# Score stacks with heads' rows interleaved by four, and the third key stack copied over its whole width

## The chip, the cores and the metric

The kernel runs on one core of a Trainium2 chip. A core has TensorE (PE, matmuls), VectorE (DVE), ScalarE (ACT), GpSimd (POOL) and SyncE (SP, which here only issues DMAs), each with its own instruction stream; they meet at semaphores. On-chip data lies in SBUF, in 128 partitions (rows); PE writes its results to PSUM, eight banks of 128 rows by 512 floats. The metric is the device time of one execution in microseconds, lower being better.

## The reference

Four graph layers follow each other over x of shape (8, 1024, 256) with a dense 1024 by 1024 adjacency per batch element; each is x = x + layer(relu(layernorm(x)), adj). The change touches only the second, eight-head attention with a head width of 32, whose scores are multiplied by twice the adjacency ahead of the softmax:

```
q, k, v = (proj(Wq, bq), proj(Wk, bk), proj(Wv, bv))      # (b, 8 heads, 1024, 32)
scores = jnp.einsum('bhqd,bhkd->bhqk', q, k) * SCALE       # SCALE = 32 ** -0.5
mask = (adj_matrix + bond_matrix)[:, None, :, :]           # both are adj
scores = scores * mask
attn = jax.nn.softmax(scores, axis=-1)
ctx = jnp.einsum('bhqk,bhkd->bhqd', attn, v)
```

All of it is float32.

## The kernel before

The program loops over the eight batch elements (batches 0 to 7); each runs the four layers in turn, with all weights and the batch's x in SBUF. Every engine has its instructions written out in order by hand; nothing is planned at run time. What follows is layer two.

**Projections.** Queries and keys are computed transposed: 128 rows of a "group" (four heads of 32 rows) by 512 columns (one half of the 1024 nodes). There are two groups and two halves, so eight projections (`project_kq`, in the order of `KQ`). ACT rounds each to the short float format that PE multiplies fast (`khi`, `qhi`), and DVE writes what is missing, again in that format (`klo`, `qlo`, `lower_kq`, L725). Semaphore `lo_s` counts the latter.

**Stacks.** A head's 32 rows don't fill PE's 128. The kernel puts four blocks of 32 rows above each other: `kS` holds khi, khi, klo, klo, and `qS` holds qhi, qlo, qhi, qlo, so that one matmul over 128 rows sums all four products of high and low parts. A head's place j in its group is head mod 4 (`HPG` is 4). For places 0, 1 and 2 the stacks are filled by DMA, from SBUF to SBUF, all issued by SP in `stack` (L446): four copies per stack (one per block), each for both groups (heads j and 4 + j) and one half of the nodes, 32 rows by 2 by 512 floats, 128 KB. For place 3 (heads 3 and 7) PE does it instead: the matrices `pick` (built once by DVE, L603) select and repeat rows in matmuls, and ACT copies the result (`LASTS`, L979).

**Order on SP, per batch:** wait for `lo_s` 2; keys (half 0) of places 0 and 1; wait for 5; keys (half 1) of place 0; wait for 6; queries (half 0) of place 0; keys (half 1) of place 1; queries (half 0) of place 1; keys of place 2, half 0, then half 1; queries (half 0) of place 2; wait for 8; queries (half 1) of places 0 to 3. That is 52 copies. Each stack has a semaphore that reaches 64 when its four copies have landed.

**Units.** A unit u is one tile of 128 queries and one head: 64 units, in the order of heads 3, 7, 0, 4, 1, 5, 2, 6 within each tile. `scores(u)` (L1202) is two matmuls of 128 by 512. In the first tile it waits for its stacks; heads 3 and 7 need no DMA, heads 0, 1 and 2 (units 2, 4, 6) wait for theirs, and heads 4, 5, 6 come with them. It also waits until DVE has read the scores of unit u - 2, which stood in the same two banks. DVE multiplies the scores by the adjacency and takes the maximum (`Z`, L787), POOL negates it (L545), ACT takes the exponential (L1002), PE transposes (L1224), ACT and DVE copy that out of PSUM (L992, L742), and PE weighs the values four heads at a time (L1252). Beside the first units PE also does two late query projections and the value projections (`BESIDE`), which ACT copies (L983). The last query projection stands behind unit 4's scores, and DVE's `lower_kq` of it ahead of DVE's `Z` of unit 4; a value projection stands behind unit 6's scores.

Of the kernel before, what the change touches and what calls it, by code (L numbers as in the profile page):

```python
# [5 lines left out]
F32 = mybir.dt.float32  # L6
# [5 lines left out]
P = 128  # L12
# [19 lines left out]
def build_program(nc, x_in, adj_in, adjT_in, mask_in, wqkT0, wv0, w1attn, bq1, bk1, bv1, bo1,  # L32
                  w1T, b1, gamma, beta, w2T, b2, w3attn, bq3, bk3, bv3, out):
    B, N, D = x_in.shape
    NT = N // P
    DT = D // P
    NH = N // HALF
# [4 lines left out]
    HD = D // HEADS  # L42
    HPG = P // HD
# [18 lines left out]
    with ctx:  # L62
# [3 lines left out]
        def signal(name, per):  # L66
            return Signal(ctx.enter_context(nc.semaphore(name)), per)
# [3 lines left out]
        ident = sb("ident", [P, P])  # L71
# [11 lines left out]
        pick = sb("pick", [P, 4, P], F32R)  # L83
# [61 lines left out]
        qS, kS = a1  # L145
# [18 lines left out]
        khi, klo, qhi, qlo, hT1, W1 = p1a  # L164
# [35 lines left out]
        x_in_s = signal("x_in_s", 32)  # L200
        out_s = signal("out_s", 16)
        x_free = signal("x_free", 1)
        kS_in = [[signal(f"kS_in{s}{j}", 64) for j in range(HPG - 1)] for s in range(NH)]
        qS_in = [[signal(f"qS_in{s}{j}", 64) for j in range(HPG - 1 + s)] for s in range(NH)]
        last_ps = signal("last_ps", len(LASTS))
        lasts = signal("lasts", len(LASTS))
# [192 lines left out]
        @block.sync  # L399
        def _(sp):  # L400
            def load(dst, src):
                sp.dma_start(dst, src).then_inc(weights_in.sem, 16)

            def load_x(b):
                sp.dma_start(xn[:], x_in[bass.ds(b, 1)].rearrange("o (t p) d -> p (o t) d", p=P)).then_inc(x_in_s.sem, 16)
                sp.dma_start(mask[:], mask_in[bass.ds(b, 1)].rearrange("o p t -> p (o t)")).then_inc(x_in_s.sem, 16)

            def load_adj(b):
                sp.dma_start(adjN[:], adj_in[bass.ds(b, 1)].rearrange("o (t p) n -> p (o t) n", p=P)).then_inc(adj_in_s.sem, 16)

            def load_w1():
                for i in range(3):
                    sp.dma_start(W1[:, i], w1attn[i].rearrange("(t p) d -> p t d", p=P)).then_inc(w1_in.sem, 16)

            def load_adjT(b):
                sp.dma_start(adjT[:], adjT_in[bass.ds(b, 1)].rearrange("o (t p) n -> p (o t) n", p=P)).then_inc(adjT_in_s.sem, 16)


            sp.sem_inc(x_free.sem, 1)
            load_x(0)  # L420
            sp.dma_start(wqk0s[:], wqkT0.rearrange("(t p) d -> p t d", p=P)).then_inc(weights0_in.sem, 16)
            sp.dma_start(W0[:, :, D:2 * D], wv0.rearrange("(t p) d -> p t d", p=P)).then_inc(weights0_in.sem, 16)
            for dst, src in ((gammac, gamma), (betac, beta), (bv1c, bv1), (bq3c, bq3), (bk3c, bk3), (bq1c, bq1),
                             (bk1c, bk1)):
                load(dst[:], src)
            load(w2s[:], w2T.rearrange("(t p) d -> p t d", p=P))
            load(Wo1[:], w1attn[3].rearrange("(t p) d -> p t d", p=P))
            for i in range(2):
                load(w3s[:, i], w3attn[i].rearrange("(t p) d -> p t d", p=P))
            for dst, src in ((bo1B, bo1), (b2B, b2), (bv3B, bv3)):  # L430
                load(dst[:], src.partition_broadcast(P))
            load_adjT(0)
            load_w1()
            load_adj(0)
            sp.wait_ge(m3_made.sem, 1)
            sp.dma_start(M3_kept, M3s[:]).then_inc(m3_kept.sem, 16)
            sp.wait_ge(m3_kept.sem, 16)

            def batch(b, last):


                def stack(dst, parts, j, cols, done):

                    for r, src in enumerate(parts):
                        to = dst[HD * r:HD * r + HD].rearrange("p (g j) n -> p g j n", j=HPG)[:, :, j, cols]
                        sp.dma_start(to.bitcast(F32), src[HD * j:HD * j + HD, :, cols].bitcast(F32)).then_inc(done.sem, 16)  # L446

                def stack_k(s, j):
                    stack(kS, (khi, khi, klo, klo), j, half(s), kS_in[s][j])

                def stack_q(s, j):
                    stack(qS, (qhi, qlo, qhi, qlo), j, half(s), qS_in[s][j])


                sp.wait_ge(*lo_s(b, 2))
                stand(sp, waited_sp)
                stack_k(0, 0)
                stack_k(0, 1)
                sp.wait_ge(*lo_s(b, 5))
                stand(sp, waited_sp)  # L460
                stack_k(1, 0)
                sp.wait_ge(*lo_s(b, 6))
                stand(sp, waited_sp)
                stack_q(0, 0)
                stack_k(1, 1)
                stack_q(0, 1)
                stack_k(0, 2)
                stack_k(1, 2)
                stack_q(0, 2)
                sp.wait_ge(*lo_s(b, 8))  # L470
                stand(sp, waited_sp)
                for j in range(HPG):
                    stack_q(1, j)

                def reload_adjT(part):
                    tiles = slice(BACK[part].start, BACK[part].stop)
                    sp.dma_start(adjT[:, tiles], adjT_in[bass.ds(b, 1)].rearrange("o (t p) n -> p (o t) n", p=P)[:, tiles]).then_inc(adjT_back[part].sem, 16)

                sp.wait_ge(*pv_ps(b, NT * GROUPS - 1))
                stand(sp, waited_sp)  # L480
                reload_adjT(0)
                sp.wait_ge(*T_ps(b, 2 * UNITS))
                stand(sp, waited_sp)
                reload_adjT(1)
                sp.wait_ge(*ctxs(b, NT))
                stand(sp, waited_sp)
                reload_adjT(2)
                sp.wait_ge(*adjT_back[2](b, 16))
                stand(sp, waited_sp)
                sp.dma_start(wB[:], adj_in[bass.ds(b, 1)][0, 0].partition_broadcast(P)).then_inc(wB_in.sem, 16)  # L490
                sp.dma_start(W1h[:], w1T.rearrange("(t p) d -> p t d", p=P)).then_inc(w2_in.sem, 16)
                sp.dma_start(W2g[:], w2T.rearrange("(t p) d -> p t d", p=P)).then_inc(w2_in.sem, 16)
                sp.dma_start(b1B[:], b1.partition_broadcast(P)).then_inc(w2_in.sem, 16)
                if not last:
                    load_w1()
                sp.wait_ge(*a3_ps(b, NT))
                stand(sp, waited_sp)
                sp.dma_start(M3[:], M3_kept).then_inc(w3_in.sem, 16)
                sp.dma_start(W3v[:, :, 0:D], w3attn[2].rearrange("(t p) d -> p t d", p=P)).then_inc(w3_in.sem, 16)
                if not last:  # L500
                    load_x(b + 1)
                    load_adj(b + 1)

                    sp.wait_ge(*p3s(b, NH * NT))
                    stand(sp, waited_sp)
                    load_adjT(b + 1)
                sp.wait_ge(*x3s(b, NT))
                stand(sp, waited_sp)
                sp.dma_start(out[bass.ds(b, 1)].rearrange("o (t p) d -> p (o t) d", p=P), x[:]).then_inc(out_s.sem, 16)
                sp.wait_ge(*out_s(b, 16))  # L510
                sp.sem_inc(x_free.sem, 1)

            with sp.Fori(0, B - 1) as b:
                batch(b, False)
            batch(B - 1, True)


# [81 lines left out]
        def _(dve):  # L599
            dve.wait_ge(consts_ready.sem, 5)  # L600
            for i, blocks in enumerate(((0, 1), (2, 3), (0, 2), (1, 3))):
                for r in range(P // HD):
                    dve.tensor_scalar(pick[:, i, HD * r:HD * (r + 1)], ident[:, P - HD:P], float(r in blocks), None,  # L603
                                      ALU.mult).then_inc(picks.sem, 1)

            def statistics(b, l, t, src):
# [466 lines left out]
        def _(pe):  # L1073
# [43 lines left out]
            def batch(b):  # L1117
# [73 lines left out]
                def scores(u):  # L1191
                    t, hd = u // HEADS, ORDER[u % HEADS]
                    if u >= 2:
                        pe.wait_ge(*zs(b, u - 1))
                    j = hd % HPG
                    if hd < HPG - 1 and t == 0:
                        for s in range(NH):
                            pe.wait_ge(*kS_in[s][j](b, 64))
                    if hd < len(qS_in[t // TPH]) and t % TPH == 0:
                        pe.wait_ge(*qS_in[t // TPH][j](b, 64))  # L1200
                    for s in range(NH):
                        mm = pe.matmul(ps[:, 2 * (u % 2) + s], qS[:, hd, rows(t)], kS[:, hd, half(s)], start=True, stop=True)  # L1202
                    mm.then_inc(S_ps.sem, 1)
# [67 lines left out]
                for u in range(STEPS):  # L1271
# [9 lines left out]
                    if u in BESIDE:  # L1281
                        what, n = BESIDE[u]
# [133 lines left out]
                for n in range(NH * NT):  # L1416
                    s, kt = n // NT, n % NT
# [4 lines left out]
                for t in range(NT):  # L1422
                    s, a = t // TPH, t % TPH
# [45 lines left out]
```

## Time and profile before

| | us |
|---|---|
| median of 3 runs | 3081.29 (3079.47 to 3081.74) |
| profiled execution, its own time | 3079.83 |
| its span, first to last instruction | 3078.0 |
| PE busy | 2976.1 (97%) |
| PE weight loads busy | 2353.4 (76%) |
| DVE busy | 1893.0 (61%) |
| ACT busy | 1473.6 (48%) |
| POOL busy | 692.9 (23%) |

Busy time is the sum of the times of an engine's instructions; PE's matmuls overlap, and their ends are modelled. Of the chain of waits that ended last, 68% of the span is PE's and 5% SP's. The hardware queue of DMAs moved 199.96 MB; 416 of its transfers are stack copies of 128 KB, 52 in each batch.

### The profile page before, as it was taken

What the parts mean: (1) busy time and instruction counts of PE and PEld (TensorE: products, weight loads), DVE (VectorE), ACT (ScalarE), POOL (GpSimd) and SP (SyncE); (2) the same over time, 40 slices, a digit from 0 to 9 for tenths busy, and PEclk for the clock granted to TensorE, in tenths of its full rate; (3) what the DMA queues carried; (4) which work ended last, traced back from release to release, by engine and by line L of the source; (5) the groups of instructions that cost most, each with busy time, mean ns of one, the idle gap of its engine ahead of it and who ended that gap; (6) DMA issues with size and microseconds to landing.
All of it is one profiled execution on the core that took longest, in us unless ns stands there. A gap on an engine that the chain in (4) does not pass through costs nothing.

```text
span 3078.0 us, 63372 instructions
## 1 busy us (share of the span) xinstructions
PE 2976.1 (97%) x22896; PEld 2353.4 (76%) x22896; DVE 1893.0 (61%) x4170; ACT 1473.6 (48%) x2729; POOL 692.9 (23%) x1241
## 2 busy tenths in 40 slices
PE   7999999999999999999999999999999999999999
PEld 6687786877878777788777887778867788677886
DVE  2698426984269742787437874378643786438863
ACT  1684217833178331783327833277322773238722
POOL 0243002430024300242002420034200342013410
PEclk9999999999999999999999999999999999999999
DMA  4302213022130231302313013121132212221200
GB/s 169 90 2 90 76 70 90 2 90 86 59 90 2 90 108 44 84 3 89 131 30 75 19 73 131 39 66 45 58 119 53 52 59 66 97 67 38 80 8 14
DMA packets 98905, 204.35 MB, mean 66 GB/s; under 512 B 11024, under 2 KB 42128, under 8 KB 98576
## 3 DMA queue, kind: packets, MB, share of 16 engines
q1 hardware_dynamic: 98576, 199.96, 20.9%
q8 instruction: 206, 3.38, 0.4%
q14 instruction: 123, 1.01, 0.1%
HBM read 136.75 MB, written 8.65 MB: 47 GB/s over the span
## 4 chain that ended last, share of the span: by engine, by line
PE 68%; issue 11%; DVE 8%; SPq 5%; POOL 4%; ACT 3%; DMA 1%; DVEq 0%; POOLq 0%; ACTq 0%
PE ps L1077 37%; PE ps L1300 11%; PE ps L1224 7%; SPq L446 4%; PE ps L1372 4%; PE ps L1252 4%; PE ps L1202 3%; POOL H L557 3%; DVE Z L787 2%; DVE stats L608 1%; DVE h L845 1%; PE ps L1114 1%; POOL nm L545 1%; ACT Z L1002 1%; DMA qS<-qlo 1%
## 5 line engine op out<-in xcount | busy, mean ns | idle before, releaser
L787 DVE CUSTOM_DVE_ANT_0 Z<-ps,adjN 128x1024 f32<-128x1024 f32 x512 | 623.8, 1218 | 69.9 <-PE ps L1202 69.9
L1002 ACT ACTIVATE Z<-Z,nm 128x1024 f32<-128x1024 f32 x512 | 587.1, 1147 | 66.7 <-POOL nm L545 66.7
L1224 PE MATMUL ps<-ident,Z 128*128 128x128 f32 x4096 | 547.8, 277 | 26.5 <-ACT Z L1002 17.6
L1224 PEld LDWEIGHTS ps<-ident,Z 128*128 128x128 f32 x4096 | 459.7, 141 | 139.3 <-issue 64.1
L1202 PE MATMUL ps<-kS,qS 128*128 128x512 f32 x1024 | 372.1, 446 | 28.4 <-DMA qS<-qlo 28.4
L534 POOL TENSOR_SCALAR ve<-mv 128x4 f32<-128x4 f32 x80 | 15.7, 196 | 1340.1 <-DVE mv L613 1339.4
L557 POOL TENSOR_SCALAR H<-adjN 128x128 fp32r<-128x128 f32 (+1 forms) x456 | 316.8, 695 | 0.0
L545 POOL TENSOR_TENSOR nm<-nm,minus 128x1 f32<-128x1 f32 x512 | 97.1, 190 | 767.4 <-DVE nm L787 762.8
L1077 PE MATMUL ps<-mh,adjT 128*128 128x256 f32 x1024 | 223.6, 379 | 0.0
L1077 PE MATMUL ps<-v,P 128*128 128x257 f32 x1024 | 223.6, 379 | 0.0
L1077 PE MATMUL ps<-hT,t3T 128*128 128x512 f32 x512 | 221.0, 592 | 0.0
L1077 PEld LDWEIGHTS ps<-v,P 128*128 128x128 f32 x1024 | 193.8, 189 | 31.9 <-issue 3.8
L1077 PEld LDWEIGHTS ps<-mh,adjT 128*128 128x128 f32 x1024 | 193.9, 190 | 26.0
L742 DVE COPY PTa<-ps 128x512 f32<-128x512 f32 x256 | 175.8, 687 | 31.9 <-PE ps L1224 31.9
L1202 PEld LDWEIGHTS ps<-kS,qS 128*128 128x128 f32 x1024 | 161.1, 192 | 39.7 <-DVE nm L787 20.4
L1077 PEld LDWEIGHTS ps<-hT,t3T 128*128 128x128 f32 x512 | 97.3, 190 | 119.1 <-issue 118.6
L1077 PE MATMUL ps<-W,hT 128*128 128x256 f32 x768 | 186.4, 395 | 0.0
L682 DVE CUSTOM_DVE_ANT_0 E<-ps,G 128x256 f32<-128x256 f32 x64 | 27.2, 424 | 245.1 <-PE ps L1077 211.0
L992 ACT ACTIVATE PTb<-ps 128x512 f32<-128x512 f32 x256 | 144.2, 588 | 59.4 <-PE ps L1224 59.4
L1077 PEld LDWEIGHTS ps<-W,hT 128*128 128x128 f32 x768 | 149.7, 200 | 25.8
L992 ACT ACTIVATE PTa<-ps 128x512 f32<-128x512 f32 x256 | 150.4, 588 | 39.1 <-PE ps L1224 39.1
L1061 ACT ACTIVATE E<-ps,cj 128x512 f32<-128x512 f32 x128 | 87.9, 687 | 159.6 <-PE ps L1077 159.6
(170 smaller groups left out, 5673.5 us busy)
## 6 DMA issues: line engine op xcount, KB each, us to landing
adjT<-adjT_in SPq DMA_DIRECT2D x8, 4096.0 KB, 13.1
adjN<-adj_in SPq DMA_DIRECT2D x8, 4096.0 KB, 17.3
adjT<-adjT_in SPq DMA_DIRECT2D x8, 2048.0 KB, 9.1
qS<-qhi SPq DMA_DIRECT2D x112, 128.0 KB, 2.5
qS<-qlo SPq DMA_DIRECT2D x112, 128.0 KB, 2.5
kS<-khi SPq DMA_DIRECT2D x96, 128.0 KB, 2.4
kS<-klo SPq DMA_DIRECT2D x96, 128.0 KB, 2.5
adjT<-adjT_in SPq DMA_DIRECT2D x8, 1536.0 KB, 12.0
```

Of the source, the lines that this page charges most:

```text
L446: sp.dma_start(to.bitcast(F32), src[HD * j:HD * j + HD, :, cols].bitcast(F32)).then_inc(done.sem, 16)
L545: pool.tensor_tensor(nm[:, u:u + 1], nm[:, u:u + 1], minus[:], ALU.mult).then_inc(nms.sem, 1)
L557: done = pool.tensor_scalar(H[:, t, of], adjN[:, t, of], 0.0, 0.0, ALU.is_equal, ALU.is_equal)
L742: dve.tensor_copy(PT(u)[:, NT // 2:NT], heads_of(ps[:, bank])).then_inc(PT_dve.sem, 1)
L787: dve.tensor_tensor_reduce(Z[:, u % ZS], ps[:, 2 * (u % 2):2 * (u % 2) + 2].rearrange("p a n -> p (a n)"), adjN[:, u // HEADS], SCORE_SCAL ...
L992: act.activation(PT(u)[:, first:first + NT // 2], heads_of(ps[:, bank]), ACT.Copy).then_inc(PT_act.sem, 1)
L1002: act.activation(Z[:, u % ZS], Z[:, u % ZS], ACT.Exp, bias=nm[:, u:u + 1], accum_out=sm[:, u:u + 1]).then_inc(exps.sem, 1)
L1077: mm = pe.matmul(dst, lhsT, rhs, start=(i == 0), stop=(i == len(pairs) - 1))
L1202: mm = pe.matmul(ps[:, 2 * (u % 2) + s], qS[:, hd, rows(t)], kS[:, hd, half(s)], start=True, stop=True)
L1224: mm = pe.transpose(ps[:, turn_bank((u, s)), rows(a)], Z[:, u % ZS, rows(NT // 2 * s + a)], ident[:])
L1252: mm = pe.matmul(ps[HD * j:HD * j + HD, 7, P * (g % GROUPS):P * (g % GROUPS + 1)], v[:, kt, HD * hd:HD * hd + HD], PT(HPG * g + j)[:, kt], ...
L1300: mm = pe.matmul(dst(n, i), lhs(n, j, i), rhs(n, j, i), start=(j == 0 and i == 0), stop=(j == NT - 1 and i == 0))
```

## The change

The rows of `wq1`, `wk1` and their biases' outputs are permuted within each group of 128: output row 4 d + j now holds dimension d of the head at place j, where row 32 j + d held it. A head's rows are thus j, j + 4, j + 8 and so on. In the stacks, block r takes the rows r, r + 4, ... in the same way. The copies step over rows by four at both ends, `pick` is written with the same step, and every stack has each head's dimensions in the same order of rows for keys and queries. The two halves of place 2's keys become one set of four copies of 32 rows by 2 by 1024 floats, 256 KB each, with one semaphore; a batch then issues 48 copies.

```
-        kS_in = [[signal(f"kS_in{s}{j}", 64) for j in range(HPG - 1)] for s in range(NH)]
+        kS_in = [[signal(f"kS_in{s}{j}", 64) for j in range(HPG - 1 - s)] for s in range(NH)]
@@ stack, on SP
                     for r, src in enumerate(parts):
-                        to = dst[HD * r:HD * r + HD].rearrange("p (g j) n -> p g j n", j=HPG)[:, :, j, cols]
-                        sp.dma_start(to.bitcast(F32), src[HD * j:HD * j + HD, :, cols].bitcast(F32)).then_inc(done.sem, 16)
+                        to = dst[r:P:HPG].rearrange("p (g j) n -> p g j n", j=HPG)[:, :, j, cols]
+                        sp.dma_start(to.bitcast(F32), src[j:P:HPG, :, cols].bitcast(F32)).then_inc(done.sem, 16)
@@ batch, on SP
                 stack_q(0, 0)
                 stack_k(1, 1)
                 stack_q(0, 1)
-                stack_k(0, 2)
-                stack_k(1, 2)
+                stack(kS, (khi, khi, klo, klo), HPG - 2, slice(0, N), kS_in[0][HPG - 2])
                 stack_q(0, 2)
@@ pick, on DVE
-                    dve.tensor_scalar(pick[:, i, HD * r:HD * (r + 1)], ident[:, P - HD:P], float(r in blocks), None,
+                    dve.tensor_scalar(pick[:, i, r:P:HPG], ident[:, HPG - 1:P:HPG], float(r in blocks), None,
                                       ALU.mult).then_inc(picks.sem, 1)
@@ scores, on PE
                         for s in range(NH):
-                            pe.wait_ge(*kS_in[s][j](b, 64))
+                            if j < len(kS_in[s]):
+                                pe.wait_ge(*kS_in[s][j](b, 64))
@@ kernel
+    def interleaved(a):
+
+        a = np.asarray(a)
+        return np.swapaxes(a.reshape(-1, P // 32, 32), -1, -2).reshape(a.shape)
+
-        "wq1": T(L1_gnn_Wq), "wk1": T(L1_gnn_Wk), "wv1": T(L1_gnn_Wv),
+        "wq1": interleaved(T(L1_gnn_Wq)), "wk1": interleaved(T(L1_gnn_Wk)), "wv1": T(L1_gnn_Wv),
-        "bq1": columns(L1_gnn_bq), "bk1": columns(L1_gnn_bk),
+        "bq1": columns(interleaved(L1_gnn_bq)), "bk1": columns(interleaved(L1_gnn_bk)),
```

## Rows read from the trace of the kernel before

**Rows 1.** The page, part 1: busy time, share and instructions of each engine
```profile
PE 2976.1 (97%) x22896; PEld 2353.4 (76%) x22896; DVE 1893.0 (61%) x4170; ACT 1473.6 (48%) x2729; POOL 692.9 (23%) x1241
```

**Rows 2.** Waits of PE over the span: total us, times, longest us
```profile
PE ps L1202 <- DMA qS<-qlo: 28.4, 16, 2.3
```

**Rows 3.** Chain of waits, 482 to 500 us: start us, us, what
```profile
491.81 2.65 DMA qS<-qlo
```

**Rows 4.** Timeline of SP, batch 1: start us, us, issue
```profile
473.60 1.25 SPq L446 DMA_DIRECT2D kS<-khi  x2
...
484.08 0.64 SPq L446 DMA_DIRECT2D qS<-qlo  x1
484.76 1.24 SPq L446 DMA_DIRECT2D kS<-khi  x2
...
491.81 0.60 SPq L446 DMA_DIRECT2D qS<-qlo  x1
```

**Rows 5.** Issues of qS, M3, adjN: duration ns min/median/max; and landings of qS
```profile
L446 SPq DMA_DIRECT2D qS<-qhi x112: 585/598/1553, 97.7 to 2781.4; - x112
DMA to landing us min/median/max: 2.3/2.5/4.0
L498 SPq DMA_DIRECT2D M<-M_kept x8: 338/339/339, 326.1 to 2986.2; - x8
L409 SPq DMA_DIRECT2D adjN<-adj_in x8: 372/838/2775, 20.6 to 2608.8; - x8
```

**Rows 6.** Timeline of PE, batch 1: start us, us, what, idle before
```profile
486.68 0.70 PE L1202 MATMUL ps<-kS,qS 128*128 128x512 f32 x2 [1.43 <-DMA qS<-qlo]
...
491.26 1.09 PE L1224 MATMUL ps<-ident,Z 128*128 128x128 f32 x8 [0.81 <-DVE PTa L742]
494.60 1.19 PE L1202 MATMUL ps<-kS,qS 128*128 128x512 f32 x2 [2.24 <-DMA qS<-qlo]
...
499.03 0.71 PE L1202 MATMUL ps<-kS,qS 128*128 128x512 f32 x2
```

**Rows 7.** Windows: us; busy PE, PEld, DVE, ACT, POOL; clock; DMA share; GB/s
```profile
110.00:120.00 10.00, 7.08 (x41) 5.46 (x40) 6.33 (x11) 5.16 (x9) 0.57 (x3) 1.00 0.84 193
490.00:500.00 10.00, 6.94 (x32) 5.46 (x32) 6.61 (x12) 4.72 (x9) 0.57 (x3) 0.83 0.87 201
870.00:880.00 10.00, 7.21 (x27) 5.99 (x28) 5.32 (x10) 4.03 (x8) 0.57 (x3) 0.66 0.87 201
```

**Rows 8.** Timeline of PE, batch 0 and then batch 2
```profile
116.40 0.70 PE L1202 MATMUL ps<-kS,qS 128*128 128x512 f32 x2 [2.10 <-DMA qS<-qlo]
...
119.45 0.72 PE L1202 MATMUL ps<-kS,qS 128*128 128x512 f32 x2
873.88 1.19 PE L1202 MATMUL ps<-kS,qS 128*128 128x512 f32 x2 [2.13 <-DMA qS<-qlo]
...
879.80 0.48 PE L1202 MATMUL ps<-kS,qS 128*128 128x512 f32 x1
```

**Rows 9.** Timeline of SP: first stack copies of batches 1 and 2
```profile
467.13 1.31 SPq L446 DMA_DIRECT2D kS<-khi  x2
846.78 1.29 SPq L446 DMA_DIRECT2D kS<-khi  x2
```

**Rows 10.** Timeline of ACT and of DVE behind unit 4's scores, batch 1
```profile
489.14 0.69 ACT L973 ACTIVATE qhi<-ps,bq1c 128x512 fp32r<-128x512 f32 x1 [2.51 <-PE ps L1077]
491.12 1.21 DVE L787 CUSTOM_DVE_ANT_0 Z<-ps,adjN 128x1024 f32<-128x1024 f32 x1
```

**Rows 11.** Windows, batch 1: stack copies, then the adjacency load
```profile
476.00:493.00 17.00, 14.11 (x71) 10.23 (x69) 9.30 (x16) 10.25 (x19) 0.95 (x5) 1.00 0.84 194
767.00:777.00 10.00, 10.00 (x47) 8.70 (x46) 2.74 (x9) 1.79 (x4) 0.00 (x0) 1.00 0.98 386
```

**Rows 12.** Groups by line: the instructions that write pick
```profile
L603 DVE TENSOR_SCALAR pick<-ident 128x32 fp32r<-128x32 f32 x16 | 1.5, 174 | 1.7 <-POOL minus L526 1.7
```

## The prediction

> **What bounds the kernel now.** I read the busy times first. PE is busy 2976.1 us of 3078.0 [rows 1], so only what PE waits for, or a lower clock, can give much back. The list of PE's waits is headed by one: the scores' matmuls wait for the copy that fills the query stack, 28.4 us in 16 waits, two in each of the eight batches [rows 2]. The chain of waits around the second of them (batch 1; batches count from 0) runs through SP's issues one after another, then 2.65 us of a DMA, then PE [rows 3]. SP's own timeline shows why: from 473.60 to 491.81 us it issues copies with 0.04 us between them, each taking about 0.60 us, so one every 0.643 us [rows 4, 5]. PE at that place has two waits [rows 6]: unit 4's scores (head 1, start 486.68, after 1.43 us idle) for the copies of `stack_q(0, 1)`, and unit 6's scores (head 2, start 494.60, after 2.24 us idle) for `stack_q(0, 2)`. I call them S4 and S6, and S7 the next unit's.
>
> Two things follow S6. First the clock: in ten microseconds around S6 the granted clock is 1.00 in batch 0, 0.83 in batches 1, 3, 5, 6 and 7, and 0.66 in batches 2 and 4 [rows 7]; that is 3.4 or 6.8 us at the lower level (1.2 instead of 2.4 GHz), which begins after PE has idled 0.81 us and then 2.24 us within a few microseconds. From S6 to S7 batch 0 takes 119.45 - 116.40 = 3.05 us, batch 1 499.03 - 494.60 = 4.43 us, batch 2 879.80 - 873.88 = 5.92 us [rows 6, 8]. So a short low stretch costs 1.38 us and a long one 2.87 us. Second, nothing behind S7 absorbs a delay: from S7 to the next batch's first stack copy it is 467.13 - 119.45 = 347.68 us in batch 0 and 846.78 - 499.03 = 347.75 us in batch 1 [rows 6, 8, 9]. Whatever S7 gains, the batch gains, one for one.
>
> **The third key stack over its whole width.** Eight issues of 128 KB (heads of place 2, two halves of four) become four of 256 KB. They stand ahead of `stack_q(0, 2)`: the last issue of `stack_q(0, 1)` starts at 484.08, then eight of kS from 484.76, then four of qS, the last at 491.81 [rows 4]. Four issues fewer, at 0.643 us: 2.57 us earlier for everything that SP issues behind. Nothing ahead of `stack_q(0, 1)` changes in number, so S4 doesn't move by this edit. Units of the second half of tiles, whose `stack_q(1, j)` come later still, have tens of microseconds in hand.
>
> S6 can't use all 2.57 us, for it also needs its PSUM bank: DVE's product of unit 4 must have read it. Behind S4 comes the last query projection, ACT's upper half of it (489.14), DVE's lower half and a copy, then DVE's product of unit 4 from 491.12 for 1.21 us [rows 10]. It ends at 492.33, and PE can start at about 492.45, that is S4 + 5.8 us. The copy now lands at 491.81 + 2.65 - 2.57 = 491.9, half a microsecond before that. So S6 goes from 494.60 to 492.45: 2.15 us in this batch; I take 2.1 for all (batch 0's wait is 2.10 [rows 8]), 8 x 2.1 = 16.8 us. What is late next is DVE's chain from S4, and the 2.24 us idle are gone but for a tenth or two.
>
> **The clock.** With that idle gone, PE's two remaining holes are the 1.43 us before S4 and the 0.81 us before the transposes at 491.26 [rows 6], with 3.8 us of matmuls between them. In all eight batches the hole before S4 is there and no low stretch follows it; in batch 0 even 0.8 and 2.1 us pass without one. I take all seven low stretches as gone: five short ones at 1.38 us and two long ones at 2.87 us = 12.6 us. Bounds: 0 (they come anyway) and 12.6.
>
> **Rows stepping by four.** The same number of copies, with the same 32 rows of two pieces each, but source and destination rows are now 0, 4, 8, ... plus an offset and not a block of 32. No copy of the trace steps over rows; bounds from the nearest. Transfer: between 476 and 493 us the DMA engines are busy 0.84 of the time and move 194 GB/s, so 231 GB/s per full share; the adjacency load, over all 128 rows, has 0.98 and 386, so 394 per full share [rows 11]. A 128 KB copy thus takes 0.57 us at the first rate and 0.33 at the second. If the stepping gives the second rate, a landing (2.5 us median [rows 5]) falls by up to 0.24 us; if not, by 0. It can't be hidden: S4 waits for it, with 1.43 us idle ahead, and what follows hangs on S4. I take 0.2, as the full-height copies in the trace all run at the faster rate: 8 x 0.2 = 1.6 us. The wide copies take 0.67 us at this rate, level with the issue, so no queue builds up.
>
> The Trainium skill bears on it: "SBUF — State Buffer", section "Door 1: The DMA port swizzle", says that 32 neighbouring partitions reach only half of the ports that DMAs use, and 128 all of them, and gives 189 against 328 GB/s for 1 MiB. This trace agrees, with 231 against 394 per full share. The same section says that partitions 32 apart share a port; each DMA engine that takes neighbouring rows of a stepped copy could then still meet another at the same port. By the first rule the sum stands; the second is rival B's, below.
>
> Issue time: 0.598 us for the stack copies; other copies issue in 0.339 (`M3`) to 0.838 us (`adjN`, median) [rows 5]. Pieces and shapes are as before, so I take the same 0.60; both ends stay in the range. With 0.34 us, S4 would lose its whole wait, 1.43 - 0.2 = 1.2 us more a batch, 10 us in all. The price of the other end is rival D's.
>
> **The rest costs nothing.** `pick` is written once by 16 DVE instructions, 1.5 us in all, of 174 ns each [rows 12], before the first statistics, with DVE waiting for inputs behind them; a doubling stays under 2 us, once, in that wait. The weights' and biases' order is changed before the launch. The projections, the six `pick` products and the scores are the same matmuls over permuted rows. PE drops one semaphore wait a batch, tens of ns. The wide copy of the third place needs both halves of the keys, which the wait ahead of `stack_q(0, 0)` has covered.
>
> **Sum.** 16.8 + 12.6 + 1.6 = 31.0 us. The profiled execution took 3079.83 us for its span of 3078.0; the sum would make it 3048.8, and the median of the runs, 3081.29, becomes 3050.3. I forecast 3050 us (**case A**, own range 3043 to 3058: 2.0 to 2.3 us of S6's wait, landing 0 to 0.24, the clock's sum two microseconds off either way, up to one more low stretch left).
>
> **Rivals.**
> B, *the transfer becomes the bound*. The stepped copies still run at 231 GB/s. A 256 KB copy then takes 1.13 us against an issue of 0.643; four leave 4 x 0.49 = 1.95 us of arrears, of which the next four small copies make up 0.3. `stack_q(0, 2)` lands 1.7 us later than in A: S6 gains 0.9 us, S4 nothing. That is 7 us, and with 1.3 us of idle left some low stretches stay; half of them gone gives 6 more: 3068 us. For it: the share of 0.84 shows the DMAs near their limit already. Against it: the full-height loads run well above it. Chance 0.13.
> C, *the clock falls anyway*. The wait goes, but low stretches of the same length come from the remaining holes: 18.4 us, 3063 us. Against it: no low stretch behind S4's wait in any batch. Chance 0.09.
> D, *slower: SP's issue of a stepped copy is dearer*. Place: the same unbroken run of issues. S6 has 24 issues ahead of it from 473.60 on instead of 28, so the change loses from 28 x 0.643 / 24 = 0.750 us an issue, that is 0.11 us more each. At `adjN`'s 0.84, so 0.24 above 0.60, `stack_q(0, 2)` comes 24 x 0.24 - 2.57 = 3.2 us later and S6 with it: 26 us slower, 3107 us; at 0.15 more it is 8 us, 3090. For it: the stack copies' 0.60 is above most others' already, so shape does count. Against it: the shape, apart from the step, is unchanged. Chance 0.07.
> E, *issue is cheaper too*: S4's wait goes as well, 3040 us. Chance 0.06.
> F, *nothing to be measured*: gains and losses of B and D cancel. Chance 0.05.
>
> **Chances.** A 0.60, B 0.13, C 0.09, D 0.07, E 0.06, F 0.05. Range 3040 to 3070 us: it takes in A, B, C and E at its edge, and leaves out D and F. A measurement of this kernel can tell 0.2% (6 us) from no change. Faster: A + B + C + E = 0.88; within 0.2%: 0.05; slower: 0.07.
>
> **What would show it.** SP: 24 issues from the wait's end to the last of `stack_q(0, 2)`, still at 0.60 us, and four kS copies of 256 KB. Landing: 2.3 us in place of 2.5; DMA share in that stretch near 0.5 at the same GB/s (B: still 0.84 or more). PE: S6 at S4 + 5.8 us instead of 7.9, waiting for DVE and no longer for a DMA; S4's wait 1.2 us. Clock 1.00 in all eight windows and S6 to S7 3.05 us everywhere (C: still 0.83 and 0.66). S7 to the next batch's first copy still 347.7 us. Wrong if the issues take 0.7 us or more, or if S7's gain is given back before the next batch begins.

## The result, and the profile after

The changed kernel takes 3049.07 us (median of 4 runs, 3048.06 to 3049.49) against 3080.85 us of the kernel before (3079.47 to 3081.74, 4 runs): a ratio of 0.9897, 95% interval 0.988 to 0.9914. The forecast was 3050 us. The profiled execution took 3049.49 us with a span of 3047.7 us, 30.3 us less than the span before; its mean granted clock is 1.000.

First the waits of PE, with total us, times and longest: the one that stood at 28.4 us in 16 waits [rows 2] is down to 10.9 us in 9, and no longer heads the list.

```profile
PE ps L1224 <- ACT Z L1001: 17.7, 64, 0.6
PE ps L1202 <- DMA qS<-qlo: 10.9, 9, 1.8
```

The timeline of PE in batch 1 (start us, us, what, idle before), beside [rows 6]: S4 still waits for its copies, S6 no longer waits for anything long enough to be shown, and S7 follows after 3.08 us.

```profile
483.82 0.70 PE L1202 MATMUL ps<-kS,qS 128*128 128x512 f32 x2 [1.52 <-DMA qS<-qlo]
...
488.40 1.09 PE L1224 MATMUL ps<-ident,Z 128*128 128x128 f32 x8 [0.82 <-DVE PTa L741]
489.54 0.73 PE L1202 MATMUL ps<-kS,qS 128*128 128x512 f32 x2
490.11 1.89 PE L1076 MATMUL ps<-W,hT 128*128 128x256 f32 x8
...
492.62 0.71 PE L1202 MATMUL ps<-kS,qS 128*128 128x512 f32 x2
```

The chain of waits after unit 4 now runs through DVE's product of unit 4, where [rows 3] had a DMA:

```profile
488.26 1.21 DVE Z L786
489.48 0.02 DVE nm L786
489.50 0.04 issue
489.54 0.73 PE ps L1202 x2
```

Windows of the same place in batches 0, 1 and 2 (us; busy of PE, PEld, DVE, ACT, POOL; clock; DMA share; GB/s), beside [rows 7], and then the run of stack copies, beside [rows 11]. The clock is 1.00 everywhere; in the run of copies the share fell from 0.84 to 0.56 while the rate rose from 194 to 215 GB/s.

```profile
107.00:117.00 10.00, 8.53 (x45) 6.37 (x46) 6.22 (x11) 5.85 (x12) 0.56 (x3) 1.00 0.64 248
486.00:496.00 10.00, 9.14 (x56) 7.66 (x55) 7.78 (x13) 7.15 (x13) 0.77 (x4) 1.00 0.51 196
863.00:873.00 10.00, 8.70 (x51) 6.90 (x49) 7.95 (x14) 7.42 (x15) 0.77 (x4) 1.00 0.51 195
...
473.00:489.00 16.00, 13.66 (x68) 10.02 (x67) 8.16 (x13) 9.95 (x18) 0.76 (x4) 1.00 0.56 215
```

SP: the issues of qS over the whole run with their landings (beside [rows 5]), and four entries of batch 1's timeline with the next batch's first (beside [rows 4, 9]). An issue costs what it did; a landing takes 2.1 us and not 2.5. One issue of batch 1 takes 1.53 us; every batch has such a long issue, before the change too (1.28 us in batch 1).

```profile
L446 SPq DMA_DIRECT2D qS<-qhi x112: 587/600/1847, 96.9 to 2752.9; - x112
DMA to landing us min/median/max: 2.0/2.1/4.1
```

```profile
470.64 1.24 SPq L446 DMA_DIRECT2D kS<-khi  x2
...
478.61 1.53 SPq L446 DMA_DIRECT2D qS<-qhi  x1
...
481.46 0.60 SPq L446 DMA_DIRECT2D qS<-qlo  x1
...
486.63 0.60 SPq L446 DMA_DIRECT2D qS<-qlo  x1
...
840.44 1.26 SPq L446 DMA_DIRECT2D kS<-khi  x2
```

Where the 30.3 us come from, by reading the same places in all eight batches. From a batch's first stack copy to S4: 156.1 us summed over the eight before, 156.1 after, a gain of 0.0. From S4 to S6: 62.9 before (7.77 to 7.96 each), 45.7 after (5.71 or 5.72 each), 17.2 gained. From S6 to S7: 37.9 before (3.05 to 5.92), 24.7 after (3.08 or 3.09 each), 13.2 gained. From S7 to the next batch's first copy: 347.2 to 347.8 before, 347.7 to 347.8 after, so 0.9 lost over the seven. The first copy of batch 0 comes 0.9 us earlier. Together 30.4 us, for 30.3.

### The profile page after: what moved, and what is told of

Read it like the earlier page. It is cut to its first block, busy times and chain, and to the rows that moved or that the text cites. A ratio compares the mean times of both kernels' runs of the same rounds, so it can differ in the third digit from the quotient of the medians.

```text
span 3047.7 us, 63332 instructions
## 1 busy us (share of the span) xinstructions
PE 2962.7 (97%) x22896; PEld 2343.5 (77%) x22896; DVE 1892.1 (62%) x4170; ACT 1474.1 (48%) x2729; POOL 694.7 (23%) x1241
## 4 chain that ended last, share of the span: by engine, by line
PE 66%; DVE 11%; issue 11%; POOL 4%; ACT 3%; SPq 3%; DMA 1%; DVEq 0%; POOLq 0%; ACTq 0%
PE ps L1076 37%; PE ps L1300 9%; PE ps L1224 7%; PE ps L1372 4%; PE ps L1252 4%; PE ps L1202 4%; SPq L446 3%; POOL H L556 3%; DVE Z L786 2%; DVE junk L828 2%; DVE stats L607 1%; DVE h L844 1%; PE ps L1113 1%; POOL nm L544 1%; ACT Z L1001 1%
## 5 line engine op out<-in xcount | busy, mean ns | idle before, releaser
L1202 PE MATMUL ps<-kS,qS 128*128 128x512 f32 x1024 | 369.5, 443 | 11.3 <-DMA qS<-qlo 10.9
L1076 PE MATMUL ps<-W,hT 128*128 128x256 f32 x768 | 176.8, 380 | 0.0
L1076 PEld LDWEIGHTS ps<-W,hT 128*128 128x128 f32 x768 | 142.5, 190 | 22.6
```

Source lines behind the costliest of these rows:

```text
L1076: mm = pe.matmul(dst, lhsT, rhs, start=(i == 0), stop=(i == len(pairs) - 1))
```

## The experiments

Ratios are against the kernel before, run on the same chip. Its median was 3080.39 us (19 runs) beside the first four experiments, and 3078.97 us (7 runs) beside the last three.

**Stepping alone** (`e1_step_only`), the changed kernel with the third place's keys in halves again (the signal and PE's wait that go with it are not shown):

```
-                stack(kS, (khi, khi, klo, klo), HPG - 2, slice(0, N), kS_in[0][HPG - 2])
+                stack_k(0, 2)
+                stack_k(1, 2)
```

> The changed kernel with place 2's key stack copied in two halves again (eight copies of 128 KB), rows still stepping by four. Theory (the gain is one wait: SP's issues ahead of S6): S6 waits for its copy as before, about 7.6 us behind S4 in place of 7.9; share of DMAs about 0.5; the low stretches of the clock stay in most batches; 3078 us, 3072 to 3082. Rival (the faster, stepped transfers bring the gain): S6 close behind DVE's chain, 3060 us or less.

3076.56 us, ratio 0.9989 (0.9979 to 0.9998): 3.8 us. Landings take 2.1 us, the share is 0.52, and still S6 waits 2.02 us, 7.7 us behind S4; six of eight batches have a low stretch. Batch 1 on PE, S4, S6 and S7:

```profile
484.58 0.70 PE L1202 MATMUL ps<-kS,qS 128*128 128x512 f32 x2 [1.30 <-DMA qS<-qlo]
...
492.27 1.19 PE L1202 MATMUL ps<-kS,qS 128*128 128x512 f32 x2 [2.02 <-DMA qS<-qlo]
496.75 0.72 PE L1202 MATMUL ps<-kS,qS 128*128 128x512 f32 x2
```

The theory holds, the rival falls: faster transfers alone bring next to nothing, since SP's issues set the pace. From the 25th to the 36th copy of a batch, the twelve that end with `stack_q(0, 2)`, issues start every 0.643 us on average and landings come every 0.645.

**Width alone** (`e2_wide_only`), the kernel before with the wide copies (signal and wait again not shown):

```
-                stack_k(0, 2)
-                stack_k(1, 2)
+                stack(kS, (khi, khi, klo, klo), HPG - 2, slice(0, N), kS_in[0][HPG - 2])
```

> The kernel before with place 2's keys in four copies of 256 KB, rows in blocks of 32 as before. Theory (at 231 GB/s a wide copy takes 1.13 us against an issue of 0.643, and four leave arrears of 1.95 us): DMA share near 1, S6 at S4 + 7.0 us, waiting for the DMA; with part of the low stretches 3068 us, 3060 to 3075. Rival (only the number of issues counts): S6 at S4 + 5.8 us, clock 1.00 everywhere, 3050 to 3053 us.

3084.39 us, ratio 1.0013 (1.0003 to 1.0022): 4.0 us slower. Both expectations miss. The direction of the first was right (S6 waits for the DMA, 8.1 to 8.4 us behind S4), but the price was too low. SP in batch 3:

```profile
1245.92 1.25 SPq L446 DMA_DIRECT2D kS<-khi  x2
1247.22 1.95 SPq L446 DMA_DIRECT2D kS<-klo  x2
1249.21 1.36 SPq L446 DMA_DIRECT2D qS<-qhi  x1
1250.62 1.32 SPq L446 DMA_DIRECT2D qS<-qlo  x1
1251.97 0.67 SPq L446 DMA_DIRECT2D qS<-qhi  x1
```

The arrears show at the DMAs first. While the wide copies run, the engines are busy 0.95 to 0.96 of the time and move 197 to 203 GB/s, in every batch. Batch 3:

```profile
1247.00:1252.00 5.00, 3.76 (x16) 2.26 (x16) 0.86 (x2) 2.77 (x5) 0.19 (x1) 1.00 0.96 200
```

At 200 GB/s a wide copy takes 1.31 us and not 1.13; the landings of the wide copies come 1.21 to 1.49 us apart (means over the batches). A small copy then takes 0.66 us, a little more than an issue. The kernel before was at this limit already: in its last twelve copies up to S6 the issues start every 0.641 us, but the landings come every 0.667. So four wide copies leave 4 x (1.31 - 0.643) = 2.7 us of arrears, the small ones behind them win none of it back, and the 2.57 us that four issues fewer save are gone.

SP feels it too: the fourth wide copy and the two issues behind it take 1.26 to 1.44 us each, about the time of one wide transfer. That SP has to wait there until a wide copy is through is a guess; `e6_step_src` below speaks against a plain limit on what may be under way. All eight batches have a low stretch, batch 1's already behind S4, where PE had waited 2.10 us.

**PE's wait filled** (`e3_fill_wait`), the kernel before with, in `scores`:

```
+                    if u == 6:
+                        for _ in range(8):
+                            pe.matmul(ps[:, 0], pick[:, 0], khi[:, 0, half(0)], start=True, stop=True)
```

> The kernel before, with eight matmuls of 128x512 put ahead of unit 6's scores, which work on data that lies there and write a bank that the scores write anew; they fill some 1.8 us of the 2.24 us that PE idles. Theory (the low stretches of the clock follow from this idle): S6 starts when it did, clock 1.00 in all windows, S6 to S7 3.05 us, 3068 us (12.6 us less). Rival (the clock falls for another reason): 0.83 and 0.66 as before and 3081 us.

3067.07 us, ratio 0.9955 (0.9939 to 0.9972): 13.3 us faster by eight useless matmuls a batch. They fill 2.13 us; what they write is overwritten by the scores. Batch 1 on PE, and the windows of batches 1 and 2:

```profile
485.25 0.70 PE L1205 MATMUL ps<-kS,qS 128*128 128x512 f32 x2 [1.65 <-DMA qS<-qlo]
...
490.97 2.13 PE L1198 MATMUL ps<-khi,pick 128*128 128x512 f32 x8
493.11 0.70 PE L1205 MATMUL ps<-kS,qS 128*128 128x512 f32 x2
...
496.17 0.71 PE L1205 MATMUL ps<-kS,qS 128*128 128x512 f32 x2
```

```profile
488.00:498.00 10.00, 9.13 (x50) 7.21 (x48) 7.62 (x12) 5.96 (x11) 0.57 (x3) 1.00 0.86 200
867.00:877.00 10.00, 9.08 (x49) 7.23 (x48) 7.61 (x13) 5.26 (x11) 0.76 (x4) 1.00 0.87 200
```

S6 is 7.86 us behind S4 (before: 7.91), S7 3.06 behind S6: the clock's part of the gain, alone. Over the eight batches S6 to S7 falls by 13.4 us. The low stretches do follow from that idle.

**The long issue** (`e4_fetch_shift`), the changed kernel with, on PE:

```
                 keep_warm(6, 3)
+                for _ in range(128):
+                    pe.wait_ge(consts_ready.sem, 5)
```

> The changed kernel with 128 semaphore waits, satisfied long ago, in PE's stream behind the dummy matmuls that keep it warm ahead of layer two. Question: in every batch one issue on SP takes 1.15 to 1.94 us in place of 0.60, at the moment when queue 8 fetches 16 KB of instructions. Theory (these are PE's instructions, and the fetch stalls SP's issue): the fetch comes some 128 instructions of PE earlier, around 13 us, ahead of SP's long run of issues; no issue in the run takes over 0.8 us, S4 comes 0.9 us earlier in each batch, 3042 us. Rival (the long issue is SP's own, at this place of its program): it stays where it is, and the time is 3049 us or, with the waits' own time, up to 3060.

3058.09 us, ratio 0.9929 (0.9912 to 0.9945), so 9.0 us slower than the changed kernel's median. The waits themselves cost 1.3 us a batch (S7 to the next first copy 349.1 us in place of 347.8), more than they were thought to. The fetch came 4.4 to 8.8 us earlier within batches 1 to 6, and 0.7 to 1.2 us earlier in batches 0 and 7, not 13; so in seven of eight batches it stays inside SP's run, and the time is in the rival's range, not at 3042 us. But the long issue moved with the fetch: from 14.4 us behind a batch's first copy to 9.2 in batch 1.

```profile
475.11 2.24 SPq L446 DMA_DIRECT2D qS<-qhi  x1
477.40 0.60 SPq L446 DMA_DIRECT2D qS<-qlo  x1
```

and the DMA queues between 475.0 and 476.5 us there (packets, MB, share):

```profile
q8 instruction: 1, 0.02, 7.9%
```

Only PE's program was lengthened, and the fetch and the long issue both followed; so the fetch is of PE's instructions, and SP's issue suffers from it. In all nine kernels' traces, 71 of 72 batches have a fetch of 16 KB on queue 8 inside the run of issues, and each overlaps an issue of over 0.85 us. The one left is batch 2 here, whose fetch began 5.7 us behind the first copy, while SP stood waiting between two issues; the next one, begun 0.8 us into the fetch, took 0.59 us. There no issue was over 0.8 us, and S4 came 18.75 us behind the first copy; with one of 2.24 us (batch 1) 20.20. That is the price, within one run.

**Stepping at one end** (`e5_step_dst`, `e6_step_src`), the changed kernel with the first edit in the former and the second in the latter. Source and destination then name different rows, so the stacks hold wrong rows and the result is not the layer's; the number, size and order of copies and matmuls are the same:

```
-src[j:P:HPG, :, cols]
+src[HD * j:HD * j + HD, :, cols]
...
-to = dst[r:P:HPG].rearrange(...)
+to = dst[HD * r:HD * r + HD].rearrange(...)
```

> The changed kernel, but the stack copies read blocks of 32 rows and only write stepped rows (so the stacks hold rows of mixed heads; the work is otherwise the same). Theory (reading and writing both go through the ports, and the slower end sets the pace): landing about 2.4 us, as with blocks at both ends; the wide copies stall SP again, S6 waits for its copy at S4 + 8 us, 3080 us. Rival (only the written end counts): landing 2.1 us, DMA share 0.55, S6 at S4 + 5.7 us, 3049 us.

> The changed kernel, but the stack copies read stepped rows and write blocks of 32 rows (the stacks then pair keys and queries of the same order still, except for the place that PE fills). Theory (the slower end sets the pace): landing about 2.4 us, SP stalled in the wide copies, 3080 us. Rival (only the read end counts): landing 2.1 us and 3049 us.

One run each: 3075.87 us with only the destination stepped, 3130.33 us with only the source stepped. Landings of qS, first the former, then the latter:

```profile
DMA to landing us min/median/max: 2.6/2.8/4.6
```

```profile
DMA to landing us min/median/max: 4.0/5.7/12.7
```

Neither end alone gives 2.1 us, so both rivals fall. These medians mix a copy's own time with its queue. The first copy of each batch has nothing ahead of it: on average it lands after 2.10 us with steps at both ends, 2.45 with blocks, 2.65 with only the destination stepped and 2.99 with only the source. So "the slower end sets the pace" is not borne out as it stands either, since both mixed forms are slower than blocks. For the destination it comes near: S6 is 7.6 to 8.5 us behind S4, SP is held up at the wide copies, and 3075.87 us lies inside the spread of the kernel before (3074.71 to 3083.13), so this one run shows no difference from it.

With only the source stepped, the landings of a batch's first eight copies already come 0.88 us apart, against issues 0.65 apart, and arrears grow until the last `stack_q(0, 2)` copy lands about 12 us after its issue. Yet SP is not held up by the wide copies there: its only long issue in that run is the one that goes with the fetch. So what held SP in e2 is not simply how much is under way, and stays open. What makes a copy between unlike patterns of rows slow stays open too; it could be which DMA engine takes which rows, but nothing here shows that.

**Four issues handed to POOL** (`e7_pool_issue`), the changed kernel without `stack_k(1, 1)` on SP and with, on POOL behind its addition of `bo1B`:

```
+                pool.wait_ge(*lo_s(b, 5))
+                stand(pool, waited_pool)
+                for r, src in enumerate((khi, khi, klo, klo)):
+                    to = kS[r:P:HPG].rearrange("p (g j) n -> p g j n", j=HPG)[:, :, 1, half(1)]
+                    pool.dma_start(to.bitcast(F32), src[1:P:HPG, :, half(1)].bitcast(F32)).then_inc(kS_in[1][1].sem, 16)
```

> The changed kernel with the four copies of place 1's second half of keys issued by POOL, which idles there, and not by SP. Theory (S4 waits for SP's run of 16 issues, each 0.643 us): 12 issues remain, `stack_q(0, 1)` lands 2.6 us earlier, S4 loses its whole wait of 1.0 to 1.8 us and everything behind it moves along, S6 still at S4 + 5.7 us: 8 x 1.3 = 10 us, 3039 us. Rival (POOL's own issues are slow, over 2.5 us each, or hold up its maxima for ACT): S4 waits for kS, no gain or slower, 3049 to 3070 us.

3036.94 us, ratio 0.9862 (0.9846 to 0.9879): the fastest of all, 12 us below the changed kernel's median (11 by the two ratios). POOL's issues and PE's S4 in batch 1:

```profile
471.89 1.22 POOL L544 DMA_DIRECT2D kS<-khi  x2 [5.27 <-DVE klo L728]
473.11 1.10 POOL L544 DMA_DIRECT2D kS<-klo  x2
```

```profile
482.81 0.71 PE L1206 MATMUL ps<-kS,qS 128*128 128x512 f32 x2
...
488.54 0.74 PE L1206 MATMUL ps<-kS,qS 128*128 128x512 f32 x2
```

S4 has no wait in any batch and comes 17.9 us behind the first copy in six of eight, where it was 19.0 to 20.1 before, after the change and in e1; S6 stays 5.73 behind it. Of PE's waits for the copies 1.2 us in 2 waits are left, both at unit 2. In those six the last copy of `stack_q(0, 1)` is issued before the long issue comes, which then falls among the wide copies and costs nothing.

## Why the prediction was right

**S6's wait: right.** 2.1 us a batch forecast, 2.15 measured, and the next bound is the one named, DVE's chain from S4 (5.8 us forecast, 5.72 measured). e1 shows that the faster copies alone don't end it, e2 that the four issues fewer alone don't either: it takes both, as the forecast had it with "no queue builds up". It names only the issue as what S6 waited for, though; the block copies, landing every 0.667 us, were as slow as the issues.

**The clock: right for this kernel.** 12.6 us forecast, 13.2 measured, and e3 shows this part by itself, 13.3 us, with the copies as they were. The two terms taken for all stretches were near enough: measured, the five short ones cost 1.4 to 1.7 us each (1.38 taken), the two long ones 2.7 and 2.9 (2.87 taken). The low level begins in part while PE still idles (batch 2: 1.0 us before S6, batch 1: 0.6), not behind the whole 2.24 us. And the term is that of one run: the 19 runs of the kernel before beside e1 to e4 took 3074.67 to 3084.29 us at mean clocks of 0.991 to 0.997, the longer ones at the lower clocks, so its sum of low stretches changes from run to run. "No low stretch follows S4's wait" is no rule, though: with 2.10 us of idle in e2's batch 1 one did.

**Stepped rows: the rate right, its gain not.** 394 GB/s per full share was assumed; 215 / 0.56 = 384 was measured, in the window from 473 to 489 us above. The landing fell by 0.4 us, more than the 0.2 taken. But the term "8 x 0.2 = 1.6 us" came out as 0.0 in this pair of profiles, as S4 didn't move. What stood against it is SP's long issue, which the prediction overlooked though [rows 5] shows a maximum of 1553 ns, and though from 473.60 to 491.81 us [rows 4] are 18.21 us, where 27 periods of 0.643 make 17.36: it averages 1.18 us a batch before (0.91 to 1.55) and 1.52 us after (1.15 to 1.94), 0.34 us more. e4 ties it to the fetch of PE's instructions. That it is longer with stepped rows is not borne out: in e3, with blocks, it averages 1.46 us, in e1, stepped, 1.47. At this equal length S4 comes 19.78 us behind the first copy in e3 and 19.41 in e1. Taking from each batch's S4 what its long issues take over 0.60 us leaves 18.9 us on average in each of before, e2 and e3 (blocks), and 18.5 to 18.6 in each of after, e1 and e4 (steps): 0.34 us for the landing, 2.7 us a run. So the term was too small, and one profile on each side hid it, by the luck of where the fetch fell.

**Passing on one for one: right.** 347.7 us from S7 to the next batch's first copy before, 347.8 after.

**Rival B: its mechanism was real, its price and its sign wrong.** It was to leave 13 us of gain at 231 GB/s. e2, which is B built, lost 4.0 us. The error is the term "1.13 us against an issue of 0.643". It took 194 GB/s at a share of 0.84 to mean 231 at a full one; at 0.96 the same copies made 200, so a wide copy takes 1.31 us and the arrears are 2.7 us and not 1.95. And the 0.3 us that the small copies should have won back isn't there, as they take 0.66 us each. The range's upper edge of 3070 us rested on this; had the stepping done nothing, the time would have been outside.

**Rivals C, D, E, F** didn't occur: clock 1.00, issues at 0.600 us.

**The number: near in part by luck.** The profiles differ by 30.3 us where the sum has 31.0, since errors cancel: S6's wait 0.4 us more than forecast, the clock 0.6 more, the landings' 1.6 us missing, 0.9 lost between the batches and 0.9 gained ahead of the first.

The two edits are worth 3.8 us and -4.0 us alone, and 31.8 us together. Two limits lay side by side, an issue every 0.643 us and a block copy every 0.66: taking away one leaves the other. The width takes four issues off SP's run but needs the rate that the stepping gives; the stepping gives a rate of which little is used until the copies are wide.

## What to carry to other kernels

Where an engine waits for the last of a row of DMAs issued back to back, price the issue (count x period) and the transfer separately and ask which one is the period; if both are near the period, removing one alone buys nothing, and merging copies helps only if the transfer of a merged one still fits into about one issue. Read a transfer's rate where the engines are really full: 0.84 busy, scaled up to 1, promised 231 GB/s where 200 came. A wait of two microseconds on PE can cost 1.4 to 2.9 us more by the clock behind it: compare the same stretch with and without the low level before the wait is priced. An idle queue on another engine is worth trying as well: it brought about 12 us on top of the change. What it would bring with block copies, which were at their rate's limit, was not run.

## What the runs showed of the hardware

- Copies within SBUF between blocks of 32 neighbouring rows ran at 194 GB/s with the DMA engines busy 0.84 of the time (231 per full share) and at 200 with them busy 0.96; between rows that step by four over all 128 at 384 per full share. The Trainium skill, "SBUF — State Buffer", section "Door 1: The DMA port swizzle", says that partitions 32 apart share a port; the worry that engines would still meet there is not borne out by this rate, which is near the 394 of the adjacency load.
- Stepping at one end only made landings slower than blocks at both: for the first copy of a batch 2.65 us (destination) and 2.99 us (source) against 2.45, and 2.10 with steps at both.
- A fetch of 16 KB of PE's instructions lengthened the DMA issue of SP that coincided with it, from 0.60 us to between 0.86 and 2.24 us.
- POOL issued a 128 KB copy of this kind in 0.55 to 0.80 us, 24 of 32 in under 0.57, about SP's 0.60; its copies landed after 2.9 us (median), SP's after 2.1.
- Low stretches of the clock around S6 (1.2 in place of 2.4 GHz) lasted 3.4 or 6.8 us. They came beside 0.8 and 2.2 us of idle on PE, and not at all once matmuls filled the second.
